# Scores of a causal attention: one pass of 256 columns for q's high and low part, with a copied low share, two chunks per bank

## The reference

```python
q, k, v = (gelu(x @ W1 + b1) @ W2 + b2 for each of q, k, v)
scores = einsum('bid,bjd->bij', q, k) / sqrt(256 * 512)
scores = scores * tril(ones)          # causal, no softmax
out = einsum('bij,bjd->bid', scores, v)
x = layernorm(x + layernorm_w_b(out))
x = layernorm(x + soft_mixture_of_experts(x))
```

## Time and profile before

| | |
|---|---|
| three executions, us | 669.99, 1278.31, 673.75 (median 673.75) |
| profiled execution, us | 669.37 (its span 667.5) |
| busy, share of the span | TensorE 94%, its weight loads 87%, VectorE 66%, ScalarE 62%, GpSimd 51% |
| mean granted TensorE clock | 0.983 |

### The profile page before, as it was taken

How to read it: one execution, slowest core, us unless ns; L and a number is a source line. 1 busy time by engine, 2 the same in 40 slices (tenths; PEclk the granted TensorE clock), 3 DMA queues, 4 the chain that set the end, 5 groups by cost and what they waited for, 6 DMA issues and landing times. The chain is left out here.

```text
span 667.5 us, 12766 instructions
## 1 busy us (share of the span) xinstructions
PE 628.5 (94%) x4228; PEld 579.4 (87%) x4228; DVE 439.5 (66%) x977; ACT 411.0 (62%) x920; POOL 339.0 (51%) x357
## 2 busy tenths in 40 slices
PE   4999999999999999999999999858999999989994
PEld 3899989989999899899898998857999999978883
DVE  4476677667676766776776777696555656246874
ACT  3664766666667567666666675436666666524675
POOL 2636566666665675666666655515333333103443
PEclk9999999999999999999999999887999999989998
DMA  7311201111012112010110110003000000031444
GB/s 214 95 33 32 64 31 34 32 59 36 31 31 63 31 31 63 31 31 31 35 60 31 32 33 1 1 0 65 1 0 0 0 0 1 1 63 51 145 153 159
DMA packets 30159, 30.22 MB, mean 45 GB/s; under 512 B 6159, under 2 KB 26029, under 8 KB 30125
## 3 DMA queue, kind: packets, MB, share of 16 engines
q1 hardware_dynamic: 29248, 29.78, 14.5%
q10 hardware_dynamic: 876, 0.01, 0.1%
HBM read 21.39 MB, written 8.39 MB: 45 GB/s over the span
## 5 line engine op out<-in xcount | busy, mean ns | idle before, releaser
L528 ACT ACTIVATE h_hi<-bank,bias_col 128x512 fp32r<-128x512 f32 x96 | 66.3, 691 | 36.7 <-PE bank L650 36.6
L451 POOL TENSOR_TENSOR h_lo<-xn_all,h_hi 128x512 fp32r<-128x512 f32 x32 | 41.3, 1292 | 80.5 <-ACT xn_all L530 80.5
L648 PE MATMUL bank<-xnT_hi,w_hi 128*128 128x512 f32 x192 | 77.6, 404 | 4.7 <-DVE xnT_lo L931 4.4
L649 PE MATMUL bank<-xnT_lo,w_hi 128*128 128x512 f32 x192 | 76.7, 400 | 0.0
L650 PE MATMUL bank<-xnT_hi,w_lo 128*128 128x512 f32 x192 | 76.4, 398 | 0.0
L937 DVE TENSOR_TENSOR h_lo<-bank,h_hi 128x512 fp32r<-128x512 f32 x64 | 44.2, 691 | 37.4 <-ACT bank L530 37.4
L994 DVE TENSOR_TENSOR state_lo<-bank,state_hi 128x512 fp32r<-128x512 f32 x57 | 39.1, 685 | 43.7 <-ACT state_hi L569 43.7
L1404 PE MATMUL bank<-xn_all,e_tok 128*128 128x257 f32 x256 | 66.4, 382 | 0.1
L1484 DVE COPY ET_all<-bank 128x256 f32 (+1 forms) x64 | 27.1, 423 | 55.0 <-PE bank L1398 54.8
L1315 ACT ACTIVATE e_tok<-bank,shift,xinv 128x256 f32<-128x256 f32 x64 | 36.0, 563 | 43.0 <-PE bank L1389 22.2
L457 POOL TENSOR_TENSOR ktok_lo<-xn_all,ktok_hi 128x512 fp32r<-128x512 f32 x32 | 38.2, 1195 | 47.2 <-ACT ktok_hi L545 47.2
(11 more groups left out here) (185 smaller groups left out, 2205.0 us busy)
## 6 DMA issues: line engine op xcount, KB each, us to landing
xn_all<-in_xT SPq DMA_DIRECT2D x16, 512.0 KB, 3.7
x_all<-in_L_attn_x SPq DMA_DIRECT2D x16, 512.0 KB, 3.5
out<-xn_all SPq DMA_DIRECT2D x16, 512.0 KB, 3.0
w_sb<-in_L_ffn_w SPq DMA_DIRECT2D x2, 512.0 KB, 5.5
xn_all<-in_L_ffn_w SPq DMA_DIRECT2D x2, 512.0 KB, 6.2
x_all<-in_L_attn_W1k SPq DMA_DIRECT2D x1, 256.0 KB, 4.2
x_all<-in_L_attn_W1q SPq DMA_DIRECT2D x1, 256.0 KB, 5.3
x_all<-in_L_attn_W2k SPq DMA_DIRECT2D x1, 256.0 KB, 5.4
```

The lines of the kernel that those rows point to most:

```text
L451: pool.tensor_tensor(h_lo[:, V_SLOT, m, :], hv[:, m, :], h_hi[:, V_SLOT, m, :].bitcast(F32), ALU.subtract).then_inc(hv_split, 1)
L528: nc.scalar.activation(h_hi[:, h_slot(j, n), m, :], ps, ACT.Gelu, bias=bias(n, m))
L648: nc.tensor.matmul(ps, w[0], xs[0], start=start, stop=False, skip_group_check=shared)
L649: nc.tensor.matmul(ps, w[0], xs[1], start=False, stop=False, skip_group_check=shared)
```

## The change

The q hiddens get a tile of their own, `hq`, in which high and low part of a chunk lie side by side (128 + 128 columns). `scores` now issues, per chunk and half of the features, one matmul of 256 columns (k's high part against q's high and low) and one of 128 (k's low part against q's high): 16 matmuls instead of 24. The product of high and low lands in columns of its own. So a bank holds two chunks: pair 0 stands in bank 4, pair 1 in a bank of the ring, as a new job S2, the third of now 15. ScalarE copies the low columns out (`copy_low`, one per pair); VectorE adds them with gamma, waits for itself, and multiplies by the mask in an operation of its own; rounding and splitting go by pairs. In the bodies each engine does pair 0 and pair 1 one after the other where it did all four chunks.

```diff
-            HK, HQ, HV, K2, V2, KT = (0, 1), (2, 3), (4, 5), (6, 7, 8, 9), (10, 13), (11, 12)
-            JOBS = 14
+            HK, S2, HQ, HV, K2, V2, KT = (0, 1), 2, (3, 4), (5, 6), (7, 8, 9, 10), (11, 14), (12, 13)
+            JOBS = 15
...
+            def score_pair(j, r):
+                ps = scores_ps if r == 0 else job_bank(j, S2)
+                return ps[:, :].rearrange("p (c s n) -> p c s n", c=2, s=2)
...
+                def copy_low(a, j, r):
+                    act.wait_ge(scores_done, 2 * a + r + 1)
+                    nc.scalar.copy(score_low[:, 2 * r:2 * r + 2, :], score_pair(j, r)[:, :, 1, :]
+                                   ).then_inc(low_copied, 1)
+
+                def round_masked(a, j, r):
+                    act.wait_ge(scores_masked, 2 * a + r + 1)
+                    nc.scalar.copy(masked_hi[:, 2 * r:2 * r + 2, :], score_pair(j, r)[:, :, 0, :]
                                    ).then_inc(masked_rounded, 1)
...
                     if attend:
-                        round_masked(a)
+                        copy_low(a, j, 0)
+                        copy_low(a, j, 1)
+                        round_masked(a, j, 0)
+                        round_masked(a, j, 1)
                     hidden(g, j, WQ1, 0)
...
-                        if job == 2:
-                            pe.wait_ge(kT_split, KB * g)
                         if job == 3:
                             pe.wait_ge(v_biased, 2 * g)
-                    if job > 3:
-                        pe.wait_ge(hkq_split, 4 * g + job - 3)
+                        if job == 6:
+                            pe.wait_ge(masked_split, 2 * g)
+                    if job == 4:
+                        pe.wait_ge(hkq_split, 4 * g + 1)
+                    if job == 5:
+                        pe.wait_ge(hkq_split, 4 * g + 2)
...
+                            nc.tensor.matmul(ps[:, half, :, :], k_hi[:, kb, toks], hq[:, p, kb, c, :, :],
+                                             start=(half == 0 and kb == 0), stop=False, skip_group_check=True)
+                            last = nc.tensor.matmul(ps[:, half, 0, :], k_lo[:, kb, toks], hq[:, p, kb, c, 0, :],
+                                                    start=False, stop=(kb == KB - 1), skip_group_check=True)
...
                 def attend_chunk(a, c, start, stop):
-                    if c == 0:
-                        pe.wait_ge(masked_split, a + 1)
                     if c % 2 == 0:
+                        pe.wait_ge(masked_split, 2 * a + c // 2 + 1)
...
+                def mask_scores(a, j, r):
+                    dve.wait_ge(low_copied, 2 * a + r + 1)
+                    ps = score_pair(j, r)
+                    for half in range(2):
+                        c = 2 * r + half
+                        last = nc.vector.scalar_tensor_tensor(out=ps[:, half, 0, :], in0=ps[:, half, 0, :],
+                                                              scalar=k_tok[:, c, D:D + 1], in1=score_low[:, c, :],
+                                                              op0=ALU.add, op1=ALU.add)
+                    last.then_inc(scores_summed, 1)
+                    dve.wait_ge(scores_summed, 2 * a + r + 1)
+                    nc.vector.tensor_tensor(ps[:, :, 0, :], ps[:, :, 0, :], causal[:, 0:2, :], ALU.mult
+                                            ).then_inc(scores_masked, 1)
+
+                def split_masked(a, j, r):
+                    dve.wait_ge(masked_rounded, 2 * a + r + 1)
+                    pair = slice(2 * r, 2 * r + 2)
+                    nc.vector.tensor_tensor(masked_lo[:, pair, :], score_pair(j, r)[:, :, 0, :],
+                                            masked_hi[:, pair, :].bitcast(F32), ALU.subtract).then_inc(masked_split, 1)
...
                     if attend:
-                        mask_scores(a)
-                        split_masked(a)
+                        mask_scores(a, j, 0)
+                        mask_scores(a, j, 1)
+                        split_masked(a, j, 0)
+                        split_masked(a, j, 1)
                     split_h(g, j, WQ1, 0)
```

More of the change, by code:

```diff
@@ L239, in build @@
             xT_hi, xT_lo = xnT_hi[0], xnT_lo[0]
-            h_hi = asb("h_hi", [P, 4, KB, GTOK], F32R)
-            h_lo = asb("h_lo", [P, 4, KB, GTOK], F32R)
+            h_hi = asb("h_hi", [P, 2, KB, GTOK], F32R)
+            h_lo = asb("h_lo", [P, 2, KB, GTOK], F32R)
+            hq = asb("hq", [P, 2, KB, GT, 2, P], F32R)
             k_hi = asb("k_hi", [P, KB, GTOK], F32R)
@@ L247, in build @@
             ktok_lo = asb("ktok_lo", [P, GT, D], F32R)
+            score_low = asb("score_low", [P, GT, P])
             masked_hi = asb("masked_hi", [P, GT, P], F32R)
@@ L325, in build @@
             scores_done = asem("scores_done")
+            low_copied = asem("low_copied")
+            scores_summed = asem("scores_summed")
             scores_masked = asem("scores_masked")
@@ L346, in build, with by_chunk, h_parts, q_chunk @@
             state_halves = state_ps[:, :].rearrange("p (k d) -> p k d", k=KB)
-            K_SLOT, V_SLOT = 0, 3
+            K_SLOT, V_SLOT = 0, 1
+            def by_chunk(ap):
+                return ap.rearrange("p (c n) -> p c n", c=GT)
             def q_slot(j):
-                return 1 + j % 2
-            def h_slot(j, n):
-                return (K_SLOT, q_slot(j), V_SLOT)[n]
+                return j % 2
+            def h_parts(j, n, m):
+                if n == WQ1:
+                    return hq[:, q_slot(j), m, :, 0, :], hq[:, q_slot(j), m, :, 1, :]
+                slot = K_SLOT if n == WK1 else V_SLOT
+                return by_chunk(h_hi[:, slot, m, :]), by_chunk(h_lo[:, slot, m, :])
+            def q_chunk(p, kb, c):
+                return hq[:, p, kb, c, 0, :], hq[:, p, kb, c, 1, :]
             tail_hi = [state_hi, h_hi[:, K_SLOT, :, 0:D], h_hi[:, K_SLOT, :, D:2 * D], h_hi[:, V_SLOT, :, 0:D]]
@@ L525, in hidden @@
                     job = (HK, HQ, HV)[n][m]
-                    act.wait_ge(hidden_done, 6 * g + job + 1)
+                    act.wait_ge(hidden_done, 6 * g + 2 * n + m + 1)
                     ps = job_bank(j, job)[:, :]
-                    nc.scalar.activation(h_hi[:, h_slot(j, n), m, :], ps, ACT.Gelu, bias=bias(n, m))
+                    nc.scalar.activation(h_parts(j, n, m)[0], by_chunk(ps), ACT.Gelu, bias=bias(n, m))
                     exact = hv[:, m, :] if n == WV1 else ps
@@ L560, in round_v @@
                     nc.scalar.copy(v_hi[:, pair, :], v_tok[:, pair, :]).then_inc(v_rounded, 1)
-                def round_masked(g):
-                    act.wait_ge(scores_masked, g + 1)
-                    nc.scalar.copy(masked_hi[:, :, :], scores_ps[:, :].rearrange("p (c n) -> p c n", c=GT)
+                def copy_low(a, j, r):
[5 more added lines that the diff above has]
+                    nc.scalar.copy(masked_hi[:, 2 * r:2 * r + 2, :], score_pair(j, r)[:, :, 0, :]
                                    ).then_inc(masked_rounded, 1)
@@ L730, in turn_k, with scores @@
                     last.then_inc(kT_done, 1)
[L732 to L737, removed]
+                def scores(a, j, p, r):
+                    if r == 0 and not (isinstance(a, int) and a == 0):
+                        pe.wait_ge(masked_split, 2 * a)
+                    pe.wait_ge(kT_split, KB * a + KB)
+                    ps = score_pair(j, r)
+                    for half in range(2):
+                        c = 2 * r + half
                         toks = slice(c * P, (c + 1) * P)
                         for kb in range(KB):
[L740 to L743, removed]
+                            nc.tensor.matmul(ps[:, half, :, :], k_hi[:, kb, toks], hq[:, p, kb, c, :, :],
+                                             start=(half == 0 and kb == 0), stop=False, skip_group_check=True)
+                            last = nc.tensor.matmul(ps[:, half, 0, :], k_lo[:, kb, toks], hq[:, p, kb, c, 0, :],
+                                                    start=False, stop=(kb == KB - 1), skip_group_check=True)
+                    last.then_inc(scores_done, 1)
                 def read_state(ba, i, c, p, stop, hi=state_hi, lo=state_lo):
                     pe.wait_ge(state_split, CB * ba + i)
-                    toks = slice(c * P, (c + 1) * P)
                     for kb in range(KB):
-                        last = split3(out_tile(c), (h_hi[:, p, kb, toks], h_lo[:, p, kb, toks]),
+                        last = split3(out_tile(c), q_chunk(p, kb, c),
                                       (hi[:, kb, :], lo[:, kb, :]), False, stop and kb == KB - 1, shared=True)
@@ L799, in chunk, with last_chunks @@
                         carry(a, ba, i)
-                def last_chunks(a, ja, ba, p):
+                def last_chunks(a, j, ja, ba, p):
                     i = GT * ja
@@ L818, in last_chunks @@
                     update(0)
-                    scores(a, p, (0, 1))
-                    scores(a, p, (2, 3))
```

(20 more changed lines are left out.)

## The result

Before: 669.76 us median of 20 executions. After: 673.85 us (671.71 to 675.12, 20 executions). The ratio is 1.0056, 95% interval 1.0041 to 1.007. By the ratio the change costs 3.8 us, by the medians 4.1, little but clear of noise. (Single executions far above the others, such as the 1278 us before, are left out of every comparison.)

What follows compares the result with a forecast made beforehand. The prediction took a sequence of VectorE and ScalarE work ahead of the split masked scores, not TensorE, as the bound. Losses of 3.9, 0.6 and some 0.3 us less a 0.3 gain made +4.5 on 671.1: 675 us, range 668 to 682.

Steps and rivals of the forecast that it cites:

- the chain: VectorE and ScalarE work from taking up the state after chunk 3 to the split masked scores; 0.30 us longer than TensorE's side.
- (a): TensorE's scores in one group: 8 wide and 8 narrow matmuls take 1.82 us, 0.81 less.
- (b): ScalarE's two copies of the low part fit its idle time and cost nothing; without that hole, 0.60 us.
- (c): VectorE's masks: per pair two additions, an own wait, a product of 0.42 us; the wait costs 0.11 us, twice per group.
- (d): Rounding and splitting in pairs: pair 0 is ready for `attend_chunk` of chunk 0 0.08 us earlier.
- (e): ScalarE's second rounding ahead of q's hidden jobs: they begin 0.71 us later, `read_state` of chunk 1 starts 0.35 us late.
- (f): Ring of banks with 15 jobs: all waits for banks stay hidden, the least cover 0.4 us.
- The sum: Whole run: ordinary groups 3.9 us, batch-beginning groups 0.6, first attended group -0.3, last chunks some 0.3; total +4.5 us.
- The full gain: Rival: TensorE bounds the kernel, so its saving in the scores is real, 13 us, giving 658 us; chance 0.06.
- The wash: Rival: pair 0's 0.08 us gain holds and chunk 1's 0.36 us cover suffices; about 670 us, chance 0.22.
- the change doesn't do what it says: Rival: a wide score matmul costs two narrow ones (0.22 us), TensorE saves nothing; 675 us, sharing the forecast's chance 0.66.
- The clock: Rival: longer TensorE stops drop its granted clock once per group, 21 us, giving 696; chance 0.06, shared with long ScalarE delays.

Runs made afterwards that it cites:

- A: Kernel before with 16 matmuls of 128 columns for the scores instead of 24, k's high part with q's low part left out: 669.12 us, ratio 0.9982.
- E: VectorE adds v's second bias ahead of the last two add_out: 662.57 us (0.9878) in the kernel before, 659.60 us (0.9833) in the changed kernel.
- B: Changed kernel without ScalarE's two low copies, VectorE adding a tile of zeros instead: 674.29 us, ratio 1.0044 to the kernel before.
- C: Changed kernel with pair 1 rounded after follow(0) and split after the state's split, not ahead of q's hidden jobs: 665.56 us, ratio 0.9915 to before.

## Why the prediction was right

**The bound.** The step that decided was to read start times instead of the 1.4 us of the earlier trace rows, and to follow what VectorE and ScalarE do between chunk 3 and the masked scores. A shows it from the side of TensorE (less work, same time), E from that of the chain (0.89 us moved out, 0.92 us per group gained).

**(a), scores.** 1.82 us forecast, 1.80 measured. A wide and a narrow matmul together take 1.80/8 = 0.225 us, though not as the 0.118+0.110 that I added: past the first pair the narrow one starts 0.18 us after the wide one and the next wide one 0.06 after that. By the rule for isolated matmuls in the Trainium skill (TensorE: Matmul & The Clock Gate, Back-to-back issue gap) I had worked out an estimate of 1.34 us before and 1.32 now; the rows have 2.63 and 1.80. The same section says that for few columns this rule counts too little where each matmul has its own weight load, and gives about 81 ns for 128 columns there; the rows agree with the direction and have 110 ns.

**(b), copies.** Free, by B; the second one ends at 171.73, the mask starts at 171.81.

**(c), (d), masks and pairs.** The product took 432 ns (0.42 taken), the mask of a pair 0.98 us as forecast. The own wait costs as its row said: line 1022 starts 0.03 us after line 1017 has ended, where an operation without a wait starts 0.08 ahead. The Trainium skill (VectorE: DVE Perf Modes, The DRAIN you can't avoid) has the semaphore at nothing extra; here it's 0.11 us. Pair 0 gave 0.17 us instead of 0.08: VectorE's split starts at 173.77 and takes 0.42, so it ends near 174.19, 12.30 us after the chain's start, as computed; but TensorE followed it by 0.05 us instead of the 0.14 that I carried over from the earlier trace rows. Why it follows faster isn't shown.

**(e), the second rounding.** The place was right, by C. The q gelus begin 174.17-171.20 = 2.97 us after the second split of k, before it was 171.75-169.50 = 2.25: 0.72 late, 0.71 forecast. Its cost, 0.35 us per group in the sum and 0.38 by the periods (26.95 forecast, 26.98 measured), came out so close partly by luck, as two errors cancelled. The state's split is done 16.00 us after the chain's start instead of 15.28, 0.72 late, as forecast. But TensorE followed it by 0.06 us instead of the 0.14 carried over, so that `read_state` began 0.28 us late and not 0.35 (0.45 later against the start of chunk 0, less the 0.17 of pair 0). And I left out the restart, another 0.10. The place of the stop was half wrong too: I took the first wait of chunk 1 to be `read_state`'s, but `chunk` waits for the preload ahead of `attend_chunk`, and 0.25 us of the waiting stand there. By the rows this adds nothing: with `attend_chunk` 0.25 us earlier, `read_state` would still have had to wait for the split that ended at 177.89. No run tests that alone.

**(f), the ring.** TensorE had no stop at the hidden jobs of q in this group, and C keeps the 15 jobs and gains.

**The sum.** +4.5 us forecast. By the traces the eleven ordinary groups lost 4.3 us (3.9 forecast) and the three that begin a batch 0.8 (0.6 forecast); the first attended group gained 0.33, 25.51 to 25.18 (0.3 forecast). That makes the 4.7 us of the loop. The end of the attention, where I had 0.3 us lost, lost 0.07: from the last group's scores to the transposes behind the attention it is 449.49-438.03 = 11.46 us, before 444.05-432.66 = 11.39. In the changed kernel:

```profile
438.03 0.41 PE L774 MATMUL bank<-hq,k_hi 128*128 128x256 f32 x1
...
449.49 1.04 PE L189 MATMUL bank<-ident,xn_all 128*128 128x128 f32 x8
```

and before:

```profile
432.66 0.31 PE L648 MATMUL bank<-h_hi,k_hi 128*128 128x128 f32 x1
...
444.05 1.03 PE L189 MATMUL bank<-ident,xn_all 128*128 128x128 f32 x8
```

The other differences of the two traces, 0.7 us more ahead of the first scores and 0.3 us less behind the attention, lie in parts that the change doesn't touch. The medians differ by 4.1 us. The 675 was above the measured 673.85 mainly because I put the sum on 671.1, and the kernel before is at 669.8 over 20 executions.

**The rivals.** The full gain fell in A. The wash fell with the two stops at chunk 1: its reason (pair 0 goes ahead) holds, its condition (the cover at chunk 1) did not. C, whose only difference is the order, has that cover, and there pair 0's 0.17 us per group is a gain (period 26.44 for 26.61). That the change doesn't do what it says fell with the 1.80 us. The clock stayed at 1.00 (2.4 GHz) in the loop in every group with stops of 0.96 us; a row of windows of the changed kernel, where PEclk is the number 1.00:

```profile
172.60:199.20 26.60, 25.71 (x180) 23.50 (x179) 18.86 (x42) 18.32 (x37) 16.09 (x17) 1.00 0.13 39
```

It fell once near the end of the attention, in both kernels, after TensorE had waited 3.1 us for v's last bias: to 0.50 in the earlier trace rows, and here to 0.51 (1.2 GHz):

```profile
435.40:438.80 3.40, 3.40 (x18) 3.40 (x18) 0.79 (x4) 1.23 (x5) 2.88 (x6) 0.51 0.00 0
```

It is in both, so it is no cost of the change. A stop of that length doesn't bring it by itself: in the kernel of A the clock stayed at 1.00 behind the same stop of 3.1 us, and fell 12 us later.

## What to carry to other kernels

An engine that is busy 94% of the span need not be the bound: look at start times for the one place per period where it stops, and follow who comes last there. Work taken off the busy engine then pays nothing, and whatever the edit puts on the chain that comes last is paid in full; shorten that chain first, and the same edit is worth what it saves (here +3.8 us as it was made, and -13.9 us with the chain shortened and the pairs reordered). When one operation is cut in two so that the first half can go ahead, place the second half behind everything that the first half was meant to hurry, on each engine's queue.

## What the runs showed of the hardware

After a stop TensorE's second 256-column matmul starts 0.22 us behind the first, instead of 0.118: a stop costs 0.10 us beyond its gap, in every stop of the rows above. A float32r matmul of 128 columns with its own weight load takes a step of 0.110 us among its like, one of 256 columns 0.118; alternating, the starts lie 0.18 and 0.06 us apart. TensorE's stops of 0.96 us in each period of 27 us did not lower its granted clock; behind one stop of 3.1 us it was at half for 3.4 us in the kernel before and in the changed one, and stayed full in A's. Of two VectorE operations, the second starts 0.03 us after the first one's end if it waits for it, and 0.08 us ahead of that end if it waits for nothing.
